# Token tiles 4 to 15 turned by VectorE out of DRAM instead of by TensorE, on one schedule over all column tiles

## The reference, cut to what matters

```
x = L0_attn_x                      # 2 x 1024 x 1024 = 16 token tiles of 128 tokens x 1024
xn = _layernorm(x, axis=-1)
s = _L0_attn_ref(xn, wq, wk, wv, wo)      # q, k, v = xn @ w; rope on q and k; causal attention
g = _silu(_L0_ffn_ref(xn, ...))           # 4-bit weights: silu(xn @ gate) * (xn @ up) @ down
x = x + s * g
```

## Time and profile before

| | us |
|---|---|
| median of 3 runs (2204.2 to 2204.58) | 2204.24 |
| the profiled execution's own time | 2204.33 |
| its span, first to last instruction | 2202.6 |
| TensorE matmuls busy | 2179.7 |
| VectorE, ScalarE, GpSimd busy | 1523.5, 1014.1, 1334.6 |

### The profile page before, as it was taken

One profiled execution on the slowest core, in us unless ns is written; L12 is line 12 of the kernel. 1 busy time (PEld: TensorE's weight loads), 2 busy tenths in 40 slices (PEclk: granted clock), 3 DMA queues, 4 the chain that ended last, 5 costly groups with the idle time before them and its releaser, 6 DMA issues.

```text
span 2202.6 us, 39253 instructions
## 1 busy us (share of the span) xinstructions
PE 2179.7 (99%) x14856; PEld 1106.4 (50%) x14856; DVE 1523.5 (69%) x2272; ACT 1014.1 (46%) x1918; POOL 1334.6 (61%) x1398
## 2 busy tenths in 40 slices
PE   7999999999999999999999999999999999999998
PEld 4555545555555555555555555444444444444443
DVE  5677767777777777777777773377858865555564
ACT  4333156666666666666666667344322221111211
POOL 4855588788878887888878888367620013332332
PEclk9999999999999999999999999999999999999999
DMA  6344212433243332333333333455359874333332
GB/s 206 99 109 101 48 33 59 74 64 59 63 76 76 68 51 71 71 73 69 59 66 66 74 52 61 72 164 172 101 163 327 277 262 149 110 110 110 110 116 89
DMA packets 296128, 230.01 MB, mean 104 GB/s; under 512 B 191664, under 2 KB 260782, under 8 KB 292868
## 3 DMA queue, kind: packets, MB, share of 16 engines
q1 hardware_dynamic: 295940, 227.51, 39.9%
HBM read 136.54 MB, written 90.78 MB: 103 GB/s over the span
## 4 chain that ended last, share of the span: by engine, by line
PE 97%; DVE 1%; ACT 1%; issue 1%; POOL 0%; DMA 0%; DVEq 0%; ACTq 0%; POOLq 0%
PE gu_ps L1183 39%; PE out_ps L1897 9%; PE qk_ps L726 9%; PE out_ps L1877 8%; PE mx_ps L1080 6%; PE sc_ps L1124 6%; PE dn_ps L1886 5%; PE dn_ps L1897 4%; PE o_ps L1146 4%; PE v_ps L709 2%; PE o_ps L1150 2%; PE sz_ps L1093 2%; PE sz_ps L1098 1%; PE tr_ps L695 1%; PE dn_ps L1889 1%
## 5 line engine op out<-in xcount | busy, mean ns | idle before, releaser
L1183 PE MATMUL gu_ps<-xT,wg 128*128 128x512 f16 x4128 | 983.7, 378 | 0.4 <-DVE h L1454 0.4
L1518 POOL TENSOR_TENSOR room<-room 128x1152 f16<-128x1152 f32 x256 | 539.2, 2106 | 40.7 <-ACT room L1232 27.8
L1183 PEld LDWEIGHTS gu_ps<-xT,wg 128*128 128x128 f16 x4128 | 367.7, 97 | 377.6 <-DVE h L1454 0.9
L1232 ACT ACTIVATE room<-sc_ps 128x512 f32<-128x512 f32 (+3 forms) x768 | 349.0, 489 | 369.1 <-PE sc_ps L1124 365.4
L2244 POOL TENSOR_TENSOR xT<-arena,xT 128x1024 f16<-128x1024 f32 x40 | 85.1, 2129 | 411.1 <-ACT xT L2012 411.1
L1513 POOL TENSOR_SCALAR_AFFINE_SELECT room<-room 128x128 f32<-128x128 f32 x512 | 143.8, 296 | 140.8 <-ACT room L1232 140.8
L1361 DVE TENSOR_REDUCE part<-mx_ps 128x2 f16<-128x1024 f32 x128 | 157.0, 1227 | 100.3 <-PE mx_ps L1080 100.2
L1361 DVE TENSOR_REDUCE shift<-mx_ps 128x2 f16<-128x1024 f32 (+3 forms) x256 | 212.8, 831 | 8.8
L726 PE MATMUL qk_ps<-xT,w 128*128 128x512 f16 x960 | 212.8, 379 | 0.0
L1124 PE MATMUL sc_ps<-arena 97*128 97x512 f16 (+3 forms) x768 | 209.7, 327 | 2.3 <-ACT room L1232 2.1
L1146 PE MATMUL o_ps<-arena,room 128*128 128x65 f16 x2240 | 191.1, 191 | 0.0
(11 more groups left out here) (181 smaller groups left out, 3203.1 us busy)
## 6 DMA issues: line engine op xcount, KB each, us to landing
hidden_scratch<-hT SPq DMA_DIRECT2D x84, 256.0 KB, 3.0
o_scratch<-room SPq DMA_DIRECT2D x64, 260.0 KB, 9.7
room<-o_scratch SPq DMA_DIRECT2D x16, 1040.0 KB, 7.7
hT_in<-hidden_scratch SPq DMA_DIRECT2D x11, 1344.0 KB, 7.5
arena<-q_scratch SPq DMA_DIRECT2D x48, 256.0 KB, 3.8
stock<-in_qw_d SPq DMA_DIRECT2D x42, 256.0 KB
down_scratch<-wd SPq DMA_DIRECT2D x84, 128.0 KB, 2.8
xin<-in_x SPq DMA_DIRECT2D x16, 512.0 KB, 4.6
```

The costliest lines, as they stand in the source:

```text
L1183: last = pe.matmul(to[:, :], wg[:, u, wp, s, cols], xT[:, xp, s, tokens], start=(s == 0 and k == 0), stop=(s == KT - 1 and k == 2))
L1232: act.activation(probs[:, r % 2, START[t] + c:START[t] + e], sc_ps[n % SC_BANKS][:, 0:e - c], ACT.Exp, scale=float(1.0 / np.sqrt(HD))).the ...
L1518: pool.tensor_tensor(p_lo[:, r % 2, c], probs[:, r % 2, c], p_hi[:, r % 2, c], ALU.subtract).then_inc(lo_done, 1)
```

## The change

For tiles 4 to 15 the normalised tile xn is stored to DRAM as float32 (`store_normed`) and comes back with features spread so that 32x32 blocks are all that is left to turn (`load_turned`, four DMAs of 32 partitions each in rows of 1 KB). VectorE transposes these blocks into x32 (`turn`, four transposes of 128x256), ScalarE rounds x32 straight into the high half of xT (`high_turned`), and the low half is a subtraction into xT: by VectorE for tiles 4 to 7 (chunk 0), by GpSimd for tiles 8 to 15 (`low_turned`). Tiles 0 to 3 are still turned by TensorE. The tables run over all 40 column tiles: tile 4 is normalised ahead of the loop, tile 7 at e = 4, tile 11 at e = 13, tile 15 at e = 23. x32 serves as the third input buffer for tile 2, the other tiles have two. In `finish` two waits of TensorE become one on a shared semaphore, and VectorE no longer waits for its own reciprocal.

```diff
-        NORM_AT = {0: 0, 2: 1, 4: 2, 5: 3}
-        TURN_AT = {3: 0, 5: 1, 7: 2, 8: 3}
+        NORM_AT = {0: 5, 2: 6, 4: 7, 7: 8, 9: 9, 11: 10, 13: 11, 17: 12, 19: 13, 21: 14, 23: 15}
+        FETCH_AT = {0: 4, 1: 5, 3: 6, 5: 7, 8: 8, 10: 9, 12: 10, 14: 11, 18: 12, 20: 13, 22: 14, 24: 15}
+        TURN_AT = {2: 4, 3: 5, 5: 6, 6: 7, 10: 8, 12: 9, 14: 10, 16: 11, 20: 12, 22: 13, 24: 14, 26: 15}
+        SPLIT_AT = {e + 1: n for e, n in TURN_AT.items()}
...
+            def store_normed(n):
+                sp.wait_ge(xn_done, n + 1)
+                sp.dma_start(xn_d[n], xn[:, n % 2, :]).then_inc(xn_stored[n % 2], 16)
+
+            def load_turned(n):
+                if n < CHT + 2:
+                    sp.wait_ge(xh_turned, CHT)
+                    sp.wait_ge(xl_turned, CHT)
+                else:
+                    sp.wait_ge(xt_turned, n - CHT - 1)
+                sp.wait_ge(xn_stored[n % 2], 16 * ((n - CHT) // 2 + 1))
+                for k in range(P // 32):
+                    sp.dma_start(xt[32 * k:32 * (k + 1), n % 2, :].rearrange("j (t c) -> j t c", c=D // 4),
+                                 xn_d[n, :, k * (D // 4):(k + 1) * (D // 4)].rearrange("(t j) c -> j t c", j=32)
+                                 ).then_inc(xt_loaded[n % 2], 16)
...
+                if e in NORM_AT:
+                    store_normed(NORM_AT[e])
+                    if NORM_AT[e] + 2 < TT:
+                        load_x(NORM_AT[e] + 2)
+                if e in FETCH_AT:
+                    load_turned(FETCH_AT[e])
                 load_tables(e)
...
-                if j in NORM_AT and tc + 1 < NCH:
-                    low_x((tc + 1) * CHT + NORM_AT[j])
+                if e in SPLIT_AT and SPLIT_AT[e] >= 2 * CHT:
+                    low_turned(SPLIT_AT[e])
...
+            def high_turned(n):
+                act.wait_ge(xt_turned, n - CHT + 1)
+                act.activation(xT[:, 0, :, n * P:(n + 1) * P], x32[:, :].rearrange("p (s t) -> p s t", s=KT), ACT.Copy
+                               ).then_inc(xTh_done, 1)
...
+            def turn(n):
+                dve.wait_ge(xt_loaded[n % 2], 64 * ((n - CHT) // 2 + 1))
+                if n == CHT:
+                    dve.wait_ge(xn_done, 3)
+                else:
+                    dve.wait_ge(xTh_done, n)
+                    dve.wait_ge(xTl_done, n)
+                for k in range(P // 32):
+                    cols = slice(k * (D // 4), (k + 1) * (D // 4))
+                    last = dve.transpose(x32[:, :].rearrange("p (s t) -> p s t", s=KT)[:, :, 32 * k:32 * (k + 1)],
+                                         xt[:, n % 2, cols].rearrange("p (i s) -> p s i", s=KT))
+                last.then_inc(xt_turned, 1)
...
+                if e in SPLIT_AT and SPLIT_AT[e] < 2 * CHT:
+                    low_turned(SPLIT_AT[e])
+                if e in TURN_AT:
+                    turn(TURN_AT[e])
+                if e in NORM_AT:
+                    norm(NORM_AT[e])
...
                 queries_keys(e)
-                if j in TURN_AT and tc + 1 < NCH:
-                    turn((tc + 1) * CHT + TURN_AT[j])
```

More of the change, by code:

```diff
@@ L241, in project_qkv @@
         xTl_done = sem("xTl_done")
+        xn_stored = [sem(f"xn_stored{i}") for i in range(2)]
+        xt_loaded = [sem(f"xt_loaded{i}") for i in range(2)]
+        xt_turned = sem("xt_turned")
         qk_ready = sem("qk_ready")
@@ L525, in scalar @@
             high_w(2)
+            spread(CHT)
             for e in range(NCH * CT):
@@ L531, in scalar @@
                     high_w(3 + j // 2)
-                if tc + 1 < NCH and j in TURN_AT:
-                    turned((tc + 1) * CHT + TURN_AT[j])
+                if e in SPLIT_AT:
+                    high_turned(SPLIT_AT[e])
                 if e >= 1:
                     high_qk(act, e - 1)
-                if tc + 1 < NCH and j in NORM_AT:
-                    spread((tc + 1) * CHT + NORM_AT[j])
-                    high_x((tc + 1) * CHT + NORM_AT[j])
+                if e in NORM_AT:
+                    spread(NORM_AT[e])
                 if tc == NCH - 1:
@@ L544, in norm @@
                 u = n % 2
-                dve.wait_ge(x_loaded[n % XB], 16 * (n // XB + 1))
+                own = xin[x_place(n)]
+                dve.wait_ge(x_loaded[x_place(n)], x_count(n))
                 for h in range(2):
-                    last = dve.bn_stats(bn[:, h, :], xin[:, n % XB, h * BANK:(h + 1) * BANK])
+                    last = dve.bn_stats(bn[:, h, :], own[:, h * BANK:(h + 1) * BANK])
                 last.then_inc(bn_done, 1)
@@ L663, in vector @@
             low_w(2)
+            norm(CHT)
             for e in range(NCH * CT):
@@ L668, in vector @@
                 if e == (NCH - 1) * CT:
[L669 to L670 removed]
+                    dve.wait_ge(xTh_done, TT)
+                    dve.wait_ge(xTl_done, TT)
                 if tc == NCH - 1:
@@ L682, in vector @@
                 tables_at(e)
-                if tc + 1 < NCH and j in NORM_AT:
-                    norm((tc + 1) * CHT + NORM_AT[j])
+                if e in SPLIT_AT and SPLIT_AT[e] < 2 * CHT:
+                    low_turned(SPLIT_AT[e])
+                if e in TURN_AT:
+                    turn(TURN_AT[e])
+                if e in NORM_AT:
+                    norm(NORM_AT[e])
         def tensor(pe, ahead):
```

59 lines of the change are left out of this document (37 added, 22 removed).

## The result

The change makes the kernel 0.2% slower: 2208.63 us median (2207.29 to 2210.74) against 2204.14, ratio 1.0021, interval 1.0013 to 1.0029. The forecast was 2197.5, with a range up to 2203. In the table of the experiments one execution of te_turns_8, of 3800.3 us at a granted clock of 0.56, is left out. The profiled execution took 2208.01 us and its span is 2206.3, against 2202.6.

What follows compares the result with a forecast made beforehand. TensorE was taken as the bound, its matmuls busy 2179.7 of 2202.6 us. From 2204.3, less 11.8 for transposes, plus 5.0 for a wait at chunk 2, came 2197.5 us; 8 in 10 range 2192.3 to 2203.

Steps and rivals of the forecast that it cites:

- The gain: On TensorE, tiles 4 to 15 lose their transposes: 12 x 0.98 = 11.8 us saved.
- Due time 74.2: Chunk 0, column tile 8: VectorE's last weight split ends at 72 to 74, room of 0 to 2 us.
- the 11.9 us of waits: VectorE's earlier waits ahead of the last weight split, 5.2 + 3.9 + 2.8, taken to cover most of 8.0 us new work.
- The turn: VectorE's four transposes of 128x256 per tile: 1.4 us, bounds 1.2 and 2.6.
- The rival of the strided transpose: VectorE's turns cost 2.6 us or more by reading every eighth element: 2207.1 to 2212; chance 0.10.
- turning point of 2.25: Turn length in us at which eight slower VectorE turns up to tile 11 use up the gain.
- The rival of the late loads: Turned loads land late through chunks 0 and 1; TensorE waits 8.5 to 16 us, 2201 to 2208.7; chance 0.15.
- Due time 87.1: Chunk 1's first column tile: tile 7's subtraction ends at 85.6; TensorE wait 0, upper bound 3 us.
- Due time 149.5: Chunk 2's start: tile 11's subtraction ends at 154.4, so TensorE waits 5 us, between 0 and 11.
- The restart: TensorE at half clock after the chunk 2 wait: 2.3 us, 2199.8 in total; left out of the sum.
- Chunk 3: From chunk 3 on everything stands as before, 6.8 us sooner; no cost.
- `finish`: Merged TensorE waits and the dropped reciprocal wait in the tail: costed at nothing.

Runs made afterwards that it cites:

- te_turns_8: The changed kernel, with TensorE turning tiles 4 to 7 as in the original and VectorE only tiles 8 to 15; 2210.75 us.
- best1: te_turns_8_run15 with tile 8 fetched at e = 8 rather than 9, and SP's run of heads' loads split over e = 20 and 21; 2195.81 us.
- pool_subtracts: The changed kernel, with GpSimd instead of VectorE subtracting tiles 4 to 7 too; 2211.79 us.
- plain_source: The changed kernel, with VectorE's transposes reading neighbouring elements instead of every eighth (computes other values, work otherwise the same); 2201.63 us.
- weights_first: run_at_15 with the splits of weight blocks 4 and 5 one column tile sooner, ahead of the normalization, their loads left in place; 2209.71 us.
- after: The changed kernel itself, as measured in the result; 2208.63 us.
- run_at_15: The changed kernel, with SP's long run of table loads at e = 15 instead of e = 13; 2203.55 us.
- te_turns_8_run15: te_turns_8 with SP's long run of table loads at e = 15 instead of e = 13; 2204.92 us.
- heads_split: run_at_15 with SP's run of 14 loads for the first heads cut in two halves, at e = 20 and e = 21; 2198.59 us.
- tail_only: The original kernel with only the two edits in `finish` (one TensorE wait instead of two, no VectorE wait for its reciprocal); 2204.06 us.

## Why the prediction was wrong

From the forecast span of 2195.8 to 2206.3 are 10.5 us: 5.9 for the two waits in chunk 0 (1.64 + 4.25), 3.25 for slow matmuls after two waits, 0.6 more at chunk 2, 1.06 in chunk 3, less 0.36 at the start.

- **The gain** of 11.8 us was right: TensorE has 192 instructions less, and best1's span is shorter by eight tiles' worth of it (7.8) and its earlier start.
- **"Due time 74.2", the step that failed.** It found the split of block 5 ending at 72 to 74 and cost it at 0; it ended at 79.6. The new work ahead of it was priced at 8.0 us and took 12.8: two turns 0.75 longer each, two subtractions of 4.2 together for 2.4, three splits half a us longer each. And this work was taken as covered by the 11.9 us of waits, though the change also makes VectorE ask for loads sooner: two new waits of 2.6 and 2.2 us for transfers stand in the stretch. That the cover is not free time shows in pool_subtracts. The price of the turn alone does not explain it: in plain_source, with a turn of 1.35 us, the split of block 5 still ended at 77.7 and TensorE waited 3.5 us. With tiles 4 to 7 turned by TensorE (te_turns_8) the wait is gone. The wait at column tile 6, for block 4, is the same thing one block earlier; the prediction set no due time for it. Whether the order of the work in chunk 0 would do it without moving turns is open, since weights_first left the loads behind.
- **The turn**, 1.4 us, measured 2.14, of which the stride is 0.79 (plain_source). The rival of the strided transpose named the right mechanism and gave it 0.10. Its price, 8 x 0.79 = 6.3 us, is near the 7.0 that plain_source gives. Its turning point of 2.25 was too high, because it stood on the forecast's other terms: with a turn of 1.35 us the kernel takes 2201.6 and not 2197.5. On a straight line between plain_source and after, an estimate, the gain is used up at about 1.6.
- **The rival of the late loads** has a range, 2201 to 2208.7, that holds the measured time, and TensorE did wait at column tile 8 and at chunk 2. Its mechanism is a small part only: in front of turns VectorE waited 3.5 us in all.
- **"Due time 87.1", tile 7**: the wait of 0 came true by luck. The subtraction ended at 92.0 and not at 85.6, and TensorE was late itself. In weights_first it became a wait of 5.2.
- **"Due time 149.5", tile 11**: the mechanism was right in every link, and run_at_15 takes this wait away, while the 4.09 us at column tile 8 stay. That the wait of 5.0 measured 5.6 is in part luck: the lateness brought out of chunk 0 was too small by about 8 us on VectorE's side and by 7.6 us on TensorE's, and the two cancel.
- **The restart** was left out, since the granted clock of the earlier trace rows reads 1.00. A stretch of 56 us nearly hides 3 us at half clock (it reads 0.97 in chunk 0 after the change); read over 3 us it shows 0.50. Its price here is 3.25 us. The slow value matmuls of the earlier trace rows that I gave as its evidence look like another thing: over their first 3 us the granted clock reads 1.00 too, and 17 matmuls in 3.00 us are 176 ns each, less than twice the 112 ns of the next 48 (row below). What makes them slow I haven't tried.
- **Chunk 3** at nothing: 1.06 us in after, and up to 6.2 in kernels that reach it sooner (te_turns_8_run15). SP's run of heads' loads lies ahead of the stores that the rounding waits for, and heads_split shows it.
- **`finish`** at nothing: right, by tail_only.

TensorE before, from 16.5 to 19.5 us, in the columns of the earlier trace rows:

```profile
16.50:19.50 3.00, 3.00 (x17) 2.13 (x16) 1.51 (x4) 1.71 (x3) 0.00 (x0) 1.00 0.98 312
```

## What to carry to other kernels

Idle time of an engine is cover only for work of its own pace: when work moves from a full engine to one with room, ask for every item in the new queue what it reads (a stride), which engine it shares a port with, and which loads it will now wait for, and compare the end with the due time of the next engine with all of them counted. Then look at the long runs of DMA issues: ten us of issues in one place cost nothing or five us, depending on whose store stands behind them, and to shift one and cut another was worth about 8 us here, against the 11.8 of the transposes moved. And price a wait of several us on TensorE with its half-clock restart.

## What the runs showed of the hardware

- VectorE's transpose of 128x256 float32 takes 408 ns from neighbouring elements and 607 ns from every eighth.
- Operations of VectorE with two inputs in SBUF and GpSimd's operations delayed each other by about what was left of the other one: a 1.26 us sum took 3.19 (2.06 us of the split were left), a 1.15 us subtraction 2.28 (1.2 us of the sum were left).
- Behind TensorE's waits of 2.9 to 9.2 us from column tile 0 to the start of chunk 3 the matmuls were slow; the granted clock read 0.50 in the row behind the wait (over 3.2 us at chunk 2 of after, over 5.7 us in te_turns_8). After waits of 1.45, 1.48, 1.57, 1.88, 2.00 and 2.60 us the next 48 matmuls took 10.52 us, as always. The start of the program is an exception in that column: behind 8.7 us without work it reads 1.00 from 8 to 12 us, though eight transposes take 1.05 us there and 0.65 later. Why is open.
